# Spectral mixing: second half of the spectrum applied before the remaining sums, and three of the sixteen sums over inputs moved to TensorE

## The reference, cut to what matters

```
x_dht = jnp.fft.fftn(x.astype(jnp.complex64), axes=(2, 3)).real
top = jnp.einsum('bixy,ioxy->boxy', x_dht[:, :, :M1, :M2], weights1)
bot = jnp.einsum('bixy,ioxy->boxy', x_dht[:, :, -M1:, :M2], weights2)
...
y = jnp.fft.ifftn(out_dht.astype(jnp.complex64), axes=(2, 3)).real
```

## Time and profile before

| | |
|---|---|
| time, 3 runs | 3127.42 us median (3127.13 to 3130.98) |
| the profiled execution: time, span | 3128.89 us, 3127.0 us |
| busy in it | PE 90%, DVE 83%, ACT 58%, POOL 60% |
| TensorE's granted clock | 0.983 of full, mean |

### The profile page before, as it was taken

How to read it: one execution, slowest core, us unless ns; L and a number is a source line. 1 busy time by engine, 2 the same in 40 slices (tenths; PEclk the granted TensorE clock), 3 DMA queues, 4 the chain that set the end, 5 groups by cost and what they waited for, 6 DMA issues and landing times. The chain is left out here.

```text
span 3127.0 us, 47044 instructions
## 1 busy us (share of the span) xinstructions
PE 2808.9 (90%) x13377; PEld 2139.4 (68%) x13405; DVE 2595.3 (83%) x3530; ACT 1818.4 (58%) x2321; POOL 1878.9 (60%) x1310
## 2 busy tenths in 40 slices
PE   0088899999999899899999889999999989989998
PEld 0037677788856668688874768678885766868886
DVE  8966988898884898898886698888887499888887
ACT  6853655666653555566665365566656364566664
POOL 2013174699970437399991327379995135549999
PEclk9999999999999999999999999999999999999999
DMA  6642001888960200688882200288885010078884
GB/s 251 249 135 75 1 0 27 204 199 196 229 177 0 75 1 0 146 205 197 210 206 68 74 1 0 64 201 196 203 208 158 30 45 0 0 182 197 195 203 113
DMA packets 124019, 384.79 MB, mean 123 GB/s; under 512 B 28469, under 2 KB 42597, under 8 KB 117258
## 3 DMA queue, kind: packets, MB, share of 16 engines
q1 hardware_dynamic: 121018, 371.55, 46.3%
q10 hardware_dynamic: 1280, 7.08, 0.8%
q0 software_dynamic: 1616, 4.90, 0.5%
HBM read 110.54 MB, written 40.65 MB: 48 GB/s over the span
## 5 line engine op out<-in xcount | busy, mean ns | idle before, releaser
L1010 POOL TENSOR_TENSOR work<-work 128x512 f32<-128x512 f32 x960 | 1311.0, 1371 | 194.4 <-DVE work L1436 124.7
L626 PE MATMUL psum<-workr,w 128*128 128x512 f32 (+1 forms) x5760 | 1355.5, 397 | 18.0 <-DMA workr<-mx_dram 6.7
L626 PEld LDWEIGHTS psum<-workr,w 128*128 128x128 f32 (+1 forms) x5760 | 1092.4, 190 | 280.2 <-DVE workr L1396 7.5
L1427 DVE SCALAR_TENSOR_TENSOR work<-psum,work 128x512 f32<-128x512 f32 x1152 | 763.8, 683 | 146.8 <-POOL work L1010 99.4
L981 POOL TENSOR_TENSOR work<-img 128x520 f32 (+1 forms) x256 | 387.0, 1543 | 275.5 <-DVE workr L1281 251.8
L585 PE MATMUL psum<-workr 128*128 128x512 f32 x2304 | 543.5, 398 | 3.1 <-DVE workr L1309 2.8
L585 PEld LDWEIGHTS psum<-workr 128*128 128x128 f32 x2304 | 433.7, 188 | 112.8 <-issue 5.8
L845 ACT CAST workr<-psum 128x650 fp32r<-128x650 f32 x128 | 90.2, 705 | 476.9 <-DVE psum L1393 369.1
L971 POOL TENSOR_TENSOR work<-work 128x1024 f32<-128x1024 f32 x40 | 112.3, 2840 | 424.7 <-DVE work L1194 424.0
L468 PE MATMUL psum<-work,taps 128*128 x1152 | 261.3, 390 | 26.1 <-DVE work L1147 13.5
L468 PEld LDWEIGHTS psum<-work,taps 128*128 128x128 bf16 x1152 | 113.5, 99 | 172.8 <-issue 42.3
(11 more groups left out here) (198 smaller groups left out, 3741.5 us busy)
## 6 DMA issues: line engine op xcount, KB each, us to landing
work<-img SPq DMA_DIRECT2D x1280, 146.2 KB, 3.2
work<-img SPq DMA_DIRECT2D x128, 292.5 KB, 4.2
work<-in_x SPq DMA_DIRECT2D x16, 2048.0 KB, 7.2
img<-in_x SPq DMA_DIRECT2D x32, 1024.0 KB, 9.7
work<-in_mixw SPq DMA_DIRECT2D x64, 512.0 KB, 5.1
out_x<-work SPq DMA_DIRECT2D x120, 256.0 KB, 4.1
workr<-mx_dram SPq DMA_DIRECT2D x64, 108.0 KB
mx_dram<-workr ACTq DMA_DIRECT2D x4, 864.0 KB, 6.9
```

Of the source, the lines that this page charges most:

```text
L626: mm = T.matmul(bank(m % 6), w5[wt][0:kr, P * n:P * n + P], ft[0:kr], start=(i == 0), stop=(i == 4))
L1010: G.tensor_tensor(acc_t[v], acc_t[v], pd_t[(9 * v + n) % 6], ALU.add).then_inc(s_acc, 1)
L1427: V.scalar_tensor_tensor(out=tile4(pd_t[m % 6]), in0=tile4(psum[:, m % 6, :]), scalar=0.0, in1=rv[:, q, y0:y0 + RT, x0:x0 + WO], op0=ALU.m ...
```

## The change

The second half of the spectrum is made ahead of DVE's seventh sum, of chunk 7, instead of ahead of its ninth. Chunks 6, 8 and 10 (`MIX_PE`) are no longer summed by DVE: POOL multiplies them, and TensorE sums them with 32 products of 64 columns each (16 inputs by two matrices `twice`), which read every 16th number of a row of the product and accumulate into the same PSUM columns as `across_halves`. ACT writes zeros into the places of `mixed` that these sums would have filled. The slots, the order of the loads, the order of DVE's chunks and the division between DVE and POOL change with it: DVE still multiplies six chunks (3 and 12 in place of 7 and 11) and POOL ten. Of 49 products in `keep_clock` during the mixing 8 are left.

```diff
-MIX_AT = (0, 1, 2, 3, 8, 1, 0, 8, 2, 3, 8, 1, 4, 5, 6, 7)
-MIX_DONE = (1, 0, 4, 2, 3, 7, 5, 6, 9, 8, 11, 10, 12, 14, 13, 15)
-MIX_DVE = (1, 4, 7, 9, 11, 14)
-MIX_POOL = (0, 2, 3, 5, 6, 8, 10, 12, 13, 15)
+MIX_AT = (0, 1, 2, 3, 8, 1, 8, 0, 3, 2, 1, 0, 4, 5, 6, 7)
+MIX_DONE = (1, 4, 0, 3, 2, 5, 7, 9, 12, 14, 11, 13, 15)
+MIX_DVE = (1, 4, 3, 9, 12, 14)
+MIX_POOL = (0, 2, 5, 6, 7, 8, 10, 11, 13, 15)
+MIX_PE = (6, 8, 10)
+NMIX = len(MIX_DONE)
...
-                for c in range(5, 12):
+                def load_again(c):
+
                     before = max(d for d in range(c) if MIX_AT[d] == MIX_AT[c])
-                    sp.wait_ge(s_mix, b * 16 + (MIX_DONE.index(before) + 1))
+                    sp.wait_ge(s_mix, b * NMIX + (MIX_DONE.index(before) + 1))
                     load_weights(c)
+
+                for c in range(5, 11):
+                    load_again(c)
                 sp.wait_ge(s_l1pe, b * L1PE + (NT + 10))
-                for c in range(12, 16):
+                for c in (12, 13):
+                    load_weights(c)
+                load_again(11)
+                for c in (14, 15):
                     load_weights(c)
...
-                keep_clock(18, 2)
+                def sum_inputs(c):
+
+                    pe.wait_ge(s_prod, b * len(MIX_POOL) + (MIX_POOL.index(c) + 1))
+                    products = wr[MIX_AT[c]].rearrange("p (n i) -> p n i", i=16)
+                    h, at = c % 8 // 4, c % 4 * 64
+                    for d in range(2):
+                        for i in range(16):
+                            T.matmul(swapped(d, h)[:, at:at + 64], cs("twice")[:, P * d:P * d + P], products[:, :, i],
+                                     start=False, stop=False)
+
+                keep_clock(8, 2)
                 pe.wait_ge(s_spec, b * 2 + 2)
-                pe.wait_ge(s_mix, b * 16 + 8)
+                pe.wait_ge(s_clean, b * len(MIX_PE) + len(MIX_PE))
+                pe.wait_ge(s_mix, b * NMIX + (MIX_DONE.index(7) + 1))
                 for h in range(2):
                     across_halves(0, h)
-                for h in range(2):
-                    keep_clock((17, 14)[h], 2)
-                    pe.wait_ge(s_mix, b * 16 + (4 * h + 12))
-                    across_halves(1, h).then_inc(s_dup, 1)
+                for c in MIX_PE:
+                    sum_inputs(c)
+                pe.wait_ge(s_mix, b * NMIX + (MIX_DONE.index(11) + 1))
+                across_halves(1, 0).then_inc(s_dup, 1)
+                pe.wait_ge(s_mix, b * NMIX + NMIX)
+                across_halves(1, 1).then_inc(s_dup, 1)
...
                         root(b, 0)
+                        act.wait_ge(s_sq0, b * NCH + NCH)
+                        for c in MIX_PE:
+                            A.copy(mixed[c // 8][:, 64 * (c % 8):64 * (c % 8) + 64], zero[:, :]).then_inc(s_clean, 1)
...
-                    if n % 8 == 0:
-                        spectrum(n // 8)
-                        v.wait_ge(s_spec, b * 2 + (n // 8 + 1))
+                    if n in (0, MIX_DONE.index(7)):
+                        spectrum(int(n > 0))
+                        v.wait_ge(s_spec, b * 2 + int(n > 0) + 1)
```

More of the change, by code:

```diff
@@ L249, in build @@
         s_w = [sem(f"s_mixw{k}") for k in range(9)]
-        s_prodv, s_prod, s_mix, s_dup, s_ost, s_gz = sem("s_prodv"), sem("s_prod"), sem("s_mix"), sem("s_dup"), sem("s_ost"), sem("s_gz")
+        s_prodv, s_prod, s_mix, s_dup, s_ost, s_gz, s_clean = sem("s_prodv"), sem("s_prod"), sem("s_mix"), sem("s_dup"), sem("s_ost"), sem("s_gz"), sem("s_clean")
         s_inv, s_inva, s_invd, s_y1, s_x2 = sem("s_inv"), sem("s_inva"), sem("s_invd"), sem("s_y1"), sem("s_x2")
```

## The result

The changed kernel took 3151.48 us (median of 4 runs, 3146.68 to 3152.51) against 3129.2 us of the kernel before (4 runs, 3127.13 to 3132.14): a ratio of 1.0063, 95% interval 1.005 to 1.0075. It is slower, by 0.6%. The profiled execution took 3146.68 us; it is one of the four, and the fastest.

The account below looks back on a forecast made before the run. It took DVE's products and sums to end each mixing before, TensorE's serial work after: 4.9 us more an image, 19.5 in four. 3128.9 + 19.5 - 1.7 = 3146.7 us profiled, 3145 median; range 3121 to 3154.

Parts of the forecast that it names:

- The term that decides: TensorE's sums of chunks 6, 8 and 10 in each mixing: 192 instructions at 113 ns, 21.7 us.
- TensorE's parts: In the mixing, from 17.45 us: `across_halves` 1.7, sums 21.7, `across_halves` 1.7, way to PSUM 0.2; end at 42.75.
- 60 ns of slack for dense and 9 for scattered ones: TensorE's sums: reading 64 columns takes 53 ns dense, 104 scattered, both below the matrix load's 113 ns.
- The gap of N / 2.4 + 2.5 ns: TensorE's sums by the skill's formula: an estimated 29 ns an instruction, 5.6 us for 192, making the change a gain.
- 1.7 was said: Stretch behind the mixing: at full clock in all images, 0.9 and 0.8 us saved where it ran slower before.
- The rival in which the clock falls among the sums: TensorE's sums partly at half clock: at most 1.9 us more an image, 3153 us; no separate chance, inside the forecast's 0.67.
- The last sum: DVE's end in the mixing: 33.3 or 35.3 us after the start, by weights landing 1.6 or 1.98 us apart.
- late landings: Weight loads in the mixing: chunk 8's land 3.6 us after 12.6, chunk 11's at 24.2 or 26.1 us.
- the terms of the sum: Whole run: 3128.9 + 19.5 for four mixings - 1.7 for the clock = 3146.7 us profiled; 3145 as median.

Follow-up runs that it names:

- e3: Changed kernel with chunk 10's sum given back to DVE, so TensorE sums only chunks 6 and 8; 3125.07 us, ratio 0.9991 to the kernel before.
- e7: Kernel before, its order, slots and loads kept, with only the sums of chunks 6, 8 and 10 moved to TensorE; 3158.4 us, ratio 1.009.
- e4: Changed kernel with chunks 8 and 10 summed on TensorE in one pass of 128 scattered columns; 3155.48 us, ratio 1.0091 to the kernel before.
- e6: e4 with its 128-column pass reading two runs of 64 neighbouring numbers, so the output differs; one execution, 3133.35 us.
- e5: e1 with 16 `keep_clock` products ahead of the first `across_halves`, 42 behind it, none between the last two; 3118.73 us, ratio 0.9963 to the kernel before.
- e2: Changed kernel with TensorE's sums reading 64 numbers in a row instead of every 16th, so the output differs; one execution, 3143.3 us.
- e1: Changed kernel with all 16 sums on DVE and the 17 and 14 `keep_clock` products back; 3127.66 us, ratio 0.9994 to the kernel before.
- e8: e5 with 9 `keep_clock` products put between the last two `across_halves`; 3120.57 us, ratio 0.9972 to the kernel before.

## Why the prediction was right

**The term that decides.** 192 x 0.113 = 21.7 us; it was 21.64. The row that gave it was the same engine, type, matrix size and number of columns elsewhere in the kernel. TensorE's parts stood where they were put: `across_halves` began 17.6 us after the start (17.45 said), L1237 at 42.84 (42.75 said). e3 makes this term shorter and e7 lets it begin later; the mixing follows to about 0.1 us in both, so it is shown and not only argued. That a repeated matrix gives no discount is shown too: all of L543's loads are there, 768 beside 768 product instructions, at L506's price.

**What sets the price of an instruction.** The prediction said that the load of the matrix sets the price and the scattered reads hide behind it, with 60 ns of slack for dense and 9 for scattered ones. e4 and e6 bear out that a price independent of the columns hides them, with less slack than I had: 2 to 3 ns. That this price is the matrix load, and not something else that every fp32 instruction pays, is argued and not shown: each of them has its load, and no run has one without. DVE's L1254 gave 53 + 51 = 104 ns for 64 scattered columns; TensorE needs an estimated 110. The Trainium skill's rule that accesses which each go to another 16-byte line lose speed (Advanced Engine Details and Errata, SBUF Cachelines) agrees with TensorE here: 1.72 ns a number at 64 bytes apart against at most 0.9 dense. No run tries another distance, so none shows that the line of 16 bytes is what counts.

The gap of N / 2.4 + 2.5 ns that the prediction takes from the Trainium skill (TensorE: Matmul & The Clock Gate, Back-to-back issue gap) is given there for a product by itself; the same section says that it under-counts at small N in a stream of loads and products. So the 113 ns contradict the prediction's use of the formula more than the page. The forecast didn't rest on it.

**The clock.** The stretch behind the mixing ran at a granted clock of 1.00 in all images, 18.75 to 18.77 us: 1.6 us back where 1.7 was said. The rival in which the clock falls among the sums did not come in the changed kernel. Its price was wrong: I gave it 1.9 us an image at most, from the share of half clock before. In e6's fourth image TensorE idled 3.21 us ahead of L532 and then ran at half clock for some 17 us (0.70 over the 28.3 us of the window), in the middle of an uninterrupted stream. Window over it and timeline of PE:

```profile
2499.90:2528.20 28.30, 26.13 (x144) 25.21 (x144) 15.46 (x11) 7.40 (x2) 14.36 (x6) 0.70 0.30 107
```

```profile
2502.05 2.48 PE L532 MATMUL psum<-work,consts 128*128 128x256 f32 x8 [3.21 <-DVE work L1241]
2504.33 13.75 PE L543 MATMUL psum<-work,consts 128*128 128x64 f32 x64
2517.88 8.57 PE L553 MATMUL psum<-work,consts 128*128 128x128 f32 x64
```

The mixing took 46.0 there instead of 35.7. Of these 10.4 us 2.2 are a late start: L1228, which makes the last of the second half of the spectrum, took 2.39 us instead of 0.17, beside a product of POOL. The other 8.2 are the instructions' own: the three lines add up to 24.8 us, and to 16.6 in the first image. The changed kernel came near this. Timeline of PE, its fourth image:

```profile
2518.04 1.97 PE L532 MATMUL psum<-work,consts 128*128 128x256 f32 x8 [2.70 <-DVE work L1232]
```

TensorE idled 2.70 us there, and 2.91 in e4's fourth image, and the clock stayed at 1.00; in e5's first image half clock followed an idle time of 2.26. So in these traces the length of the idle time alone doesn't tell whether the clock falls, and that this rival stayed away is in part luck. What it would cost among 192 products no run shows.

**DVE and POOL.** The last sum was to end at 33.3 to 35.3; it ended at 34.7, 33.2, 33.6 and, in the fourth image, 36.3. The fourth is a thing that the prediction hadn't: POOL's first product started 0.2 us ahead of DVE's, and DVE's first took 3.22 us instead of 1.22. The same happens in the fourth image of e2, e4, e6 and e7, and in no other. In e2 and e4 the mixing is as long (44.4). Timelines of DVE and POOL:

```profile
2500.20 3.22 DVE L1228 TENSOR_TENSOR work<-work 128x1024 f32<-128x1024 f32 x1 [0.29 <-DVE work L1219]
```

```profile
2500.00 5.64 POOL L996 TENSOR_TENSOR work<-work 128x1024 f32<-128x1024 f32 x2 [96.43 <-DVE work L1219]
```

That put off the second half (16.7 instead of 15.0), sum 7, and with it TensorE: mixing 44.57. In e6 the second half came at 15.0 all the same, since DVE's third product took 1.22 us there and not the 2.97 of the changed kernel. POOL's waits for weights were 22.1 us in 17 cases, where the trace before has 0.7 in one; the prediction had worked out late landings.

**What it left out.** It priced the three sums taken off DVE and the new order together and never asked which of them DVE's earlier end came from. e1, e5 and e8 answer: all of it from the order. Their last of sixteen sums ended after 32.8 to 34.6 us, the last of thirteen in the changed kernel after 33.2 to 36.3. In the old order three sums less were worth about 1 us (e7, 35.6 against 36.7 before). A likely reason, which no run isolates: in front of its last sum DVE waits for weights and for POOL, and those waits stay when sums go. So the change put 21.6 us on TensorE's road in each image and DVE got nothing for it.

**The size.** 3145 was said, 3151 measured, inside the range. The profiled execution, against which the sum was made, came out at 3146.68 where 3146.7 was said. That close a match is partly chance: the fourth image's 1.7 was missed, and unchanged stretches took 2.1 less. The prediction took 1.5 off for the median because the traced execution before lay above its runs; the traced execution after lies 4.5 to 5.8 below the other three. So of the 22.3 us between the medians the terms of the sum account for some 18, and the rest is not explained.

## What to carry to other kernels

A fp32 product on TensorE of up to 128 dense columns had one price in these traces, 112 to 115 ns an instruction: take the rate from a row with the same type, matrix and columns, multiply by the number of instructions (two for one product of fp32), and lay the block on that engine's own road before looking at what it relieves. Before moving work off an engine, check with the order alone whether that engine's end depends on this work or on what it waits for. And look at what `keep_clock` products stand in front of: 14 of them ahead of the last `across_halves` cost e1 most of what its order had gained (mixings 2.1 us shorter than before in sum, against 10.8 in e5), while 9 in e8 cost nothing.

## What the runs showed of the hardware that was not expected

TensorE reads fp32 columns that lie 64 bytes apart at 1.72 ns each (e4, 128 columns, 220 ns an instruction), dense ones at 0.9 or less (e6, 115 ns). An instruction, half of a fp32 product, of 64 or 128 dense columns takes 112 to 115 ns (e2, e6).

A DVE instruction of 0.17 us took 2.39 beside a product of POOL (e6, fourth image).

Once the clock had fallen (e6, fourth image, 1.3 us after the end of an idle time of 3.21 us), an uninterrupted stream of fp32 products of 64 scattered columns stayed at half clock for its 13.75 us, 215 ns an instruction, and the clock rose again only in the first microseconds of the 128-column ones. In e6's other images the same stream, entered at full clock after an idle time of 1 us, stayed at full clock. The one case doesn't say whether the kind of product is the cause.
